# Visiting the four diagonal 32x32 tiles in turn in three products of a delta-rule stage

## What is computed

```
attn = -(kb @ k.T), strictly lower triangle of a 32x32 chunk
attn = inverse of (I - attn), row by row
u = attn @ v_chunk
w = attn @ kb_chunk
then over the 16 chunks: u_new = u - w @ S;  o = q @ S + a @ u_new;  S = S + k.T @ u_new
```

## Time and profile before

| | |
|---|---|
| median of 3 runs | 2591.12 us (2587.27 to 2595.66) |
| the profiled execution | 2581.11 us, its span 2579.3 us |
| TensorE matmuls | 1943.3 us busy, 75% of the span, 22054 records |
| ScalarE | 1387.3 us, 54% |
| VectorE | 1351.0 us, 52% |
| GpSimd | 553.8 us, 21% |
| mean granted clock of TensorE | 0.866 of full |

### The profile page before, as it was taken

One profiled execution on the slowest core, in us unless ns is written; L12 is line 12 of the kernel. 1 busy time (PEld: TensorE's weight loads), 2 busy tenths in 40 slices (PEclk: granted clock), 3 DMA queues, 4 the chain that ended last, 5 costly groups with the idle time before them and its releaser, 6 DMA issues.

```text
span 2579.3 us, 53778 instructions
## 1 busy us (share of the span) xinstructions
PE 1943.3 (75%) x22054; PEld 1184.7 (46%) x22054; DVE 1351.0 (52%) x3132; ACT 1387.3 (54%) x3607; POOL 553.8 (21%) x613
## 2 busy tenths in 40 slices
PE   4239656888769777888779786888778876977777
PEld 3014344546444554446444454446444544456444
DVE  5133446554554737464654647374655556473553
ACT  1154525764476616763476527673476537672534
POOL 2710205030221105030312004030413023110230
PEclk9659867998889978998789878998799878997999
DMA  9203360002000100002000201002100201000000
GB/s 275 61 3 94 102 165 13 3 1 51 10 10 2 38 15 17 3 1 51 13 6 2 50 10 9 3 1 51 18 3 1 51 10 10 2 8 13 1 1 5
DMA packets 129890, 76.26 MB, mean 30 GB/s; under 512 B 76082, under 2 KB 121610, under 8 KB 127596
## 3 DMA queue, kind: packets, MB, share of 16 engines
q1 hardware_dynamic: 125548, 66.51, 10.6%
q0 software_dynamic: 4096, 6.32, 2.0%
HBM read 41.71 MB, written 33.16 MB: 29 GB/s over the span
## 4 chain that ended last, share of the span: by engine, by line
PE 38%; issue 23%; DVE 15%; ACT 12%; POOL 6%; another core or an unknown queue 3%; SPq 2%; DMA 1%; DVEq 0%; POOLq 0%; ACTq 0%
PE PS L1292 4%; PE PS L1433 4%; PE PS L596 3%; POOL area_b L1740 2%; DVE work_a L975 2%; PE PS L488 2%; ACT work_a L814 2%; PE PS L1325 2%; PE PS L1444 2%; PE PS L752 2%; PE PS L568 2%; DVE area_b L1625 2%; PE PS L1402 2%; PE PS L1364 1%
## 5 line engine op out<-in xcount | busy, mean ns | idle before, releaser
L1740 POOL TENSOR_TENSOR area_b<-area_b,tables 128x256 f32<-128x256 f32 x256 | 213.0, 852 | 761.7 <-DVE area_b L1625 761.7
L797 ACT ACTIVATE work_a<-PS,work_a 128x512 bf16<-128x512 f32 (+3 forms) x512 | 265.2, 543 | 132.7 <-DVE work_a L924 119.9
L924 DVE TENSOR_REDUCE work_a<-PS 128x2 f32<-128x1024 f32 (+3 forms) x256 | 201.4, 820 | 148.1 <-PE PS L488 86.5
L488 PE MATMUL PS<-strip,pick 64*128 64x128 bf16 (+4 forms) x2560 | 250.7, 277 | 0.0
L1529 ACT ACTIVATE area_b<-PS,neg_max 128x192 f32<-128x192 f32 (+1 forms) x512 | 202.3, 421 | 75.9 <-DVE neg_max L1665 58.6
L814 ACT ACTIVATE work_a<-PS 128x1024 f32<-128x1024 f32 (+1 forms) x192 | 169.4, 882 | 113.4 <-PE PS L488 112.9
L1292 PE MATMUL PS<-wqkv,area_b 128*128 128x512 f32 x384 | 201.9, 659 | 9.1 <-DVE area_b L1625 8.7
L534 PE MATMUL PS<-work_a 64*128 64x512 bf16 (+3 forms) x512 | 77.7, 345 | 159.1 <-ACT work_a L797 119.5
L1325 PE MATMUL PS<-area_b 64*128 64x192 f32 (+1 forms) x1024 | 141.6, 405 | 68.8 <-ACT area_b L1529 53.8
L596 PE MATMUL PS<-work_a 128*64 128x512 f32 (+3 forms) x1024 | 188.9, 471 | 4.0 <-ACT work_a L814 4.0
L1754 POOL TENSOR_TENSOR rstd_b<-var_eps_b,minus_half 128x4 f32<-128x4 f32 x16 | 16.4, 1025 | 786.5 <-DVE var_eps_b L120 786.5
(11 more groups left out here) (310 smaller groups left out, 4107.5 us busy)
## 6 DMA issues: line engine op xcount, KB each, us to landing
work_a<-stack_d SPq DMA_DIRECT2D x32, 512.0 KB
stack_d<-area_b SPq DMA_DIRECT2D x48, 192.0 KB, 3.3
stack_d<-area_b SPq DMA_DIRECT2D x32, 128.0 KB, 2.7
area_b<-in_L_attn_x_dram SPq DMA_DIRECT2D x4, 512.0 KB, 6.4
slots_in<-work_a SPq DMA_DIRECT2D x8, 256.0 KB, 4.9
stack_d<-work_a SPq DMA_DIRECT2D x4, 512.0 KB, 7.3
work_a<-xnT_d SPq DMA_DIRECT2D x8, 256.0 KB
work_a<-in_L_attn_x_dram SPq DMA_DIRECT2D x8, 256.0 KB
```

What stands on the lines that cost most here:

```text
L488: return nc.tensor.matmul(to, pick16[half_rows(e), half * P:(half + 1) * P], rows, start=False, stop=True, tile_position=(64 * e, 0), skip ...
L797: nc.scalar.activation(dump0[:, n % 2 * T:n % 2 * T + (i + 1) * P], PS[:, a:a + (i + 1) * P], ACT.Exp, bias=neg_max0[:, k:k + 1], accum_ou ...
L924: nc.vector.reduce_max(neg_max0[:, 2 * g * NT + i:(2 * g + 2) * NT:NT], at[:, :, Q_AT[i]:Q_AT[i] + (i + 1) * P], AX_X, negate=True).then_i ...
L1740: nc.gpsimd.tensor_tensor(to[:, n, :, r, :], src[:, n, :, 1 - r, :], table(2 * n + 1, t)[:, 32 * r:32 * r + 32].unsqueeze(1).to_broadcast( ...
```

## The change

`chunks()` gets a flag. With `in_place=True`, which the three diagonal products pass, the loop over the four chunks c of a block t of 128 tokens is innermost and the head h outside it; without it the order is as before. The set of matmuls, their operands, their tiles and the semaphores are the same, and the last matmul of each product still carries the signal.

```diff
-        def chunks():
-            for n in range(NCH):
-                t, c = divmod(n, 4)
-                for h in range(H1):
-                    yield slice(32 * c, 32 * c + 32), (t * H1 + h) * CH, slice(32 * h, 32 * h + 32), n * CH, \
+        def chunks(in_place=False):
+            for t in range(NT):
+                for a in range(16):
+                    h, c = divmod(a, 4) if in_place else (a % 4, a // 4)
+                    yield slice(32 * c, 32 * c + 32), (t * H1 + h) * CH, slice(32 * h, 32 * h + 32), (4 * t + c) * CH, \
                         t * P + h * DH1
...
-            for rc, blk, _, _, _ in chunks():
+            for rc, blk, _, _, _ in chunks(in_place=True):
                 last = nc.tensor.matmul(PS[rc, blk:blk + CH], level[rc, blk:blk + CH],
...
-            for rc, blk, _, _, _ in chunks():
+            for rc, blk, _, _, _ in chunks(in_place=True):
                 last = nc.tensor.matmul(PS[rc, BANK + blk:BANK + blk + CH],
...
-            for rc, blk, _, _, feat in chunks():
+            for rc, blk, _, _, feat in chunks(in_place=True):
                 last = nc.tensor.matmul(PS[rc, 2 * blk:2 * blk + 2 * CH].rearrange("p (n c) -> p n c", n=2),
```

## The result

| | before | after |
|---|---|---|
| median | 2589.19 us (4 runs, 2577.15 to 2595.66) | 2547.83 us (4 runs, 2542.62 to 2550.91) |
| profiled execution | 2581.11 us | 2550.84 us |
| TensorE matmuls busy | 1943.3 us | 1889.6 us |
| mean granted clock | 0.866 | 0.867 |

The ratio is 0.9853, with a 95% interval of 0.9824 to 0.9882: the kernel is 1.5% faster. The two profiled executions differ by 30.3 us, the medians by 41 us. The changed kernel was timed once more in the experiments (e4), with 0.9854 (0.9827 to 0.9882). Against the 2591.12 us from which the forecast was made, the ratio gives 2553 us; the forecast was 2561, from 2548 to 2577.

A forecast was written before the change was run, and what follows sets the result against it. TensorE's chain L681, L1393, L689, L1402 was taken as the bound. Savings of 28.4 us (batches 1 to 7), 0 (L699 there), 1.5 (batch 0) and 0 (clock) made 30, from 2591.1 to 2561 us; 80% range 2548 to 2577.

The forecast's parts named there:

- The rate of the first two products: L681 and L689: 13.4 ns a pair, taken from L740, in place of 31; each product 1.94 us.
- The path of batches 1 to 7: L681 through L1393 and L689 to L1402: 4.55 us saved a batch, 4.05 after instruction stalls, 28.4 us over seven.
- The supply of instructions: Faster L681 and L689 wait for the next instruction block: 0.5 us a batch, ends 0 and 1.5.
- fall into L1402 and are hidden by it: Instruction fetches after the stall in the first two products fall into L1402, 5 us for 32 pairs, costing nothing.
- The third product: L699 falls from 4.4 to 1.5 us, but batches 1 to 7 gain nothing (0 to 0.3 us), awaiting VectorE.
- The bank rule: In the three products, row tiles sharing one PSUM bank might be kept apart, leaving the time at the median; given 2%.
- Batch 0: L681 and L689 gain nothing there, a store being awaited; L699 is on the path and saves 1.5 us (0 to 2.9).
- The clock: The rise to 2.4 GHz in L1402 moves with it: 0 us, bounded by 12 us over seven batches either way.
- The rival in which the kernel gets slower because TensorE is less occupied: Full clock returns later, so L1402, L1433 and L1444 run slower: 26 us more, 2617 us; chance 5%.

The follow-up runs named there:

- e4: The changed kernel timed once more, nothing altered, against the kernel before; ratio 0.9854 (0.9827 to 0.9882), median 2539.7 us.
- e3: The changed kernel with neighbouring matmuls alternating between two tiles instead of four; ratio 0.9874 (0.9850 to 0.9898) to the kernel before.
- e9: The changed kernel with the 64 matmuls of L681 issued twice in a row; ratio 0.9985 (0.9963 to 1.0007) to the kernel before.
- e1: The changed kernel with the third product, L699, left in its old order; ratio 0.9845 (0.9818 to 0.9871) to the kernel before, median 2540.3 us.
- e2: The kernel before with only the third product, L699, put in the new order; ratio 0.9995 (0.9979 to 1.0011), median 2576.4 us.
- e8: The changed kernel with L699's neighbouring matmuls writing into banks 0 and 1 in turn; one execution, the product still takes 1.99 us.
- e5: The changed kernel with 12 overwritten matmuls of 512 columns ahead of L681 in batches 1 to 7; ratio 0.9865 (0.9842 to 0.9888) to the kernel before.

## Why the prediction was right, and where not

**The rate of the first two products: right.** 13.4 ns a pair and 1.94 us were taken from L740; 1.93 us was measured, at the same clock of 0.50. The row nearest in form, in tile pattern and in clock gave the length to 1%. The reasoning about tiles that I built on such rows in e3's expectation failed; the row itself did not. L714, which differs from L699 in its tile pattern, was a worse neighbour: 1.5 us were taken from it, 1.99 measured. That cost the forecast nothing, since L699 ends in a wait, but TensorE's busy time fell by 53.7 us and not by 60.

**The path of batches 1 to 7: right.** L1402 starts 4.11 us sooner after L681 (9.51 to 5.40); the forecast was 4.05. The gaps in the two products that this includes are 3.6 us in all, 3.5 were taken. L1393 and the copy behaved as worked out.

**The supply of instructions: right in kind, a little short in size.** I took 0.5 us a batch, 3.5 in all, with ends of 0 and 1.5. The gaps in L679, L687 and L1400 are 5.2 us. They did not spread over the batches: batch 7 paid 2.6 us and batch 3 2.1, above the end of 1.5, and four batches nothing. L728 lost another 2.5 us by its gaps and L697 in batch 6 0.8, for which the sum had no term. One comparison of the prediction was also wrong: 4.2 us a block would not hide the 4.39 that it read. In the old order a block spans L1393 too, 120 x 0.031 + 1.26 = 5.0 us, and that is why no gap was there. The fetches that "fall into L1402 and are hidden by it" were not always hidden: batch 3 waited 1.64 us in it. The rule "Instruction fetch mechanics" of the Trainium skill's "Runtime: NRT & Kernel Launch", that the issue rate hides the fetch, does not hold in e9: the first block there is late by 2.37 us.

**The third product: right.** It was to give nothing beyond batch 0, and e1 and e2 show that.

**The bank rule**, that different row tiles cannot access one bank at the same time ("PSUM — Partial Sum Buffer" of the Trainium skill), shows no effect on time: the products that go round four row tiles in one bank take about half of their former time, and two banks in turn for the third (e8) change nothing.

**Batch 0: right in size.** 1.5 us were forecast, 2.2 measured to the end of L728 and 0.5 before it.

**The clock: the step that failed.** "I expect the rise to move with L1402, and take 0 for it." In six of seven batches it did not move with L1402 but came well ahead of where that would put it; only in batch 7, behind two gaps, it came 2.9 us into L1402. In batch 1 the clock is up 5.4 us after the start of L681, where L1400 had hardly begun; in batches 3 and 4 it is up 3.3 and 3.2 us after it, when L687 has hardly begun. L1402 then takes 4.35 us in place of 5.70, 1.35 us a batch or 9.4 us that the sum lacked. Against that stand 0.42 us a batch in L1433, because in five batches the clock now stays down for 6.8 us around it in place of 3.4; 0.45 in L728, of which 0.35 are gaps of the instruction supply and not the clock; and the 3.9 us outside. Within the profiles these cancel, which is why 30.2 us agree with the 30 forecast. That agreement is luck in part, and better than the working. The rival in which the kernel gets slower because TensorE is less occupied had the sign of the clock's answer wrong in the products, and right behind L699.

**The size of the whole.** The repeated comparison gives 1.46% or 38 us, with 30 to 45 by its interval; the 30 of the sum lie at its edge. What makes up the difference is not traced through. The clock is one part: in e4's profile, 41 us shorter than that of the kernel before, it had not fallen at all ahead of L681 in batches 1 and 6, and the first product takes 1.28 us there. Profiles of the same kernel differ by several us, in where the clock rises and where the blocks end. From the start of the first L681 to that of the last, the two profiles of the changed kernel have 1953.3 and 1947.7 us (e4).

## What to carry to other kernels

Matmuls too small to fill the array should not follow one another in the same tile: already two tiles in turn brought 31 ns a pair down to 17, and four to 13. Before counting such a gain, ask what stands behind each product: two of these three were followed by more TensorE work and gave everything, the third was followed by a wait for VectorE and gave nothing. And when a stream of small instructions gets faster than about 4 us for 256 of them, look for gaps put down to "issue" that are a fixed number of instructions apart. Here a block of 256 came every 3.8 to 4.4 us at best, and what a higher clock gave the fast products (e5) went into such gaps for the greater part.

## What was not expected of the hardware

- The granted clock came back sooner with the new order. Before, TensorE was busy through L681, L1393 and L689 for 9.6 us and the clock stayed at 0.50; after, it was busy for some 5.2 us and the clock rose at the latest just behind L687 in six of seven batches. The number of matmuls was the same, so busy time in the records does not tell when the clock comes back. The order of the first two products does not fix it either: in e1, which has the same ones, it rose 3.1 to 9.4 us after the start of L681. What decides is open.
- In one tile the pairs of a product go at 31 ns on the lower clock and (2.73 - 0.19) / 127 = 20.0 ns on the higher, where one record takes 0.19 us; round four tiles, at 13.3 and (1.29 - 0.19) / 127 = 8.7 ns. Two tiles are already at 16.7 ns on the lower clock.
- A block of 256 instructions came 3.8 us after the last one in e9 and 4.39 us in the earlier trace rows. The packet that brings it starts only when TensorE is in the block ahead of it, so these 4 us are the time of one round and no share of a busy queue: the queue's packets fill 0.5% of the span.
